# Cross-attention over heads on one Trainium2 core: rows ordered by token pairs, scores of 32x32 blocks, probabilities transposed by VectorE and placed on zeroed diagonals by ScalarE

## The chip, the cores and the metric

The kernel runs on one core of a Trainium2 chip. The metric is the device time of one execution in microseconds, the median of several runs. Of the core's engines the text speaks of TensorE (PE; its weight loads are PEld), VectorE (DVE), ScalarE (ACT), GpSimd (POOL) and SyncE (SP), which issues most DMAs.

## What is computed

4096 tokens of 512 numbers. For each token, attention runs over its own 16 heads: a 16x16 matrix of scores between the heads of the query and those of the key, a softmax over it, and a weighted sum of the value's heads. Tokens don't see each other. A layer of eight experts, two for each token, and a shared feed-forward part follow.

```python
Q = (q @ Wq.T + bq).reshape(bs, sl, H, HD)      # H, HD = 16, 32
K = (k @ Wk.T + bk).reshape(bs, sl, H, HD)
V = (v @ Wv.T + bv).reshape(bs, sl, H, HD)
score = jnp.einsum('bshd,bsgd->bshg', Q, K)
weight = jax.nn.softmax(score, axis=-1)
attn = jnp.einsum('bshg,bsgd->bshd', weight, V).reshape(bs, sl, nf)
return attn @ Wo.T + bo
...
x = x + xattn(layernorm(x), ctx, ctx, ...)
x = x + ffn(layernorm(x), ...)
```

## The kernel before

The code is written in blocks for each engine, with semaphores set by hand; each engine's order is the order of its code. The attention stage is a loop of 16 passes (NB) of 256 tokens (two halves s of 128). The passes are staggered: pass i projects keys, queries and values of block i + 1 (names K, Q, V, "ahead"), makes the attention of block i (S, T, P), and projects, adds and normalises what block i - 1 attended (O, Z, L, "behind"). PSUM banks are handed on through semaphores full and drained. Every matmul is recorded under the helper's line 728.

Scores. A query or key is split into three f16 parts of 32 rows, and rows 96 to 103 of q_st and k_st hold a mask, so that one matmul of 104 rows by 128 columns by 128 columns gives the scores of 8 tokens (GT) with all heads, and those between different tokens are pushed far down. 32 such matmuls make a pass, in 8 steps S00 to S13 of four. They stand between the pieces of the key and query projections (line 868 and on). VectorE takes the own token's score by a maximum over the 8 (line 1465), subtracts the row maximum; ScalarE takes the exponential; VectorE divides (line 1480, pr). GpSimd spreads pr to 128x128 with zeros outside the own token (line 1980, spread, 8 instructions a pass), TensorE transposes it (line 825, 32 a pass), ScalarE copies it to spread_t (line 1171, 8 a pass), and TensorE multiplies with v_p (attend, 32 matmuls on tiles of 32 columns, each recorded as two).

SyncE's queue in a pass (line 576): 16 loads of v_p from value_rows (line 518), which first wait until the store of value_rows has landed and P1 of the last pass is done; a piece of weights to be weighed; behind the wait for S13 (line 581) and k_low, 12 moves k_parts to k_st and, behind q_low, 12 moves q_parts to q_st (line 488); then x_sb, x_res, x_rows, z_rows, z_columns, the store of the next value_rows (line 505) and the load cx_in. All are issued in this order by one queue, and a wait holds up what stands behind it. Scores of pass i + 1 need k_st and q_st from pass i.

In the last pass SyncE issues, between the value store and the last v_p loads, the loads of the weights of the shared part (wsgu_in, wsdn_in) and of its first inputs. TensorE then begins the shared part, whose weights' low halves VectorE makes in the last pass (line 1509).

## Time and profile before

| | us |
|---|---|
| median of 3 runs (1491.32 to 1495.39) | 1491.42 |
| the profiled execution | 1494.03 |
| its span | 1492.3 |
| PE busy | 1404.3 (94%) |
| DVE busy | 911.3 (61%) |
| ACT busy | 647.1 (43%) |
| POOL busy | 503.7 (34%) |
| one pass of the attention loop, attend to attend | 36.33 |

The profile is one execution. Its timelines list instructions of one engine in order of time, with runs of the same instruction merged; a group's busy time is the union of its instructions. SyncE's rows (SPq) are the issues of DMAs, not their transfers. Attention lies between about 50 and 630 us, the shared part and the experts behind it.

### The profile page before, as it was taken

What the parts mean: (1) busy time and instruction counts of PE and PEld (TensorE: products, weight loads), DVE (VectorE), ACT (ScalarE), POOL (GpSimd) and SP (SyncE); (2) the same over time, 40 slices, a digit from 0 to 9 for tenths busy, and PEclk for the clock granted to TensorE, in tenths of its full rate; (3) what the DMA queues carried; (4) which work ended last, traced back from release to release, by engine and by line L of the source; (5) the groups of instructions that cost most, each with busy time, mean ns of one, the idle gap of its engine ahead of it and who ended that gap; (6) DMA issues with size and microseconds to landing.
All of it is one profiled execution on the core that took longest, in us unless ns stands there. A gap on an engine that the chain in (4) does not pass through costs nothing.

```text
span 1492.3 us, 33015 instructions
## 1 busy us (share of the span) xinstructions
PE 1404.3 (94%) x10387; PEld 1070.7 (72%) x10388; DVE 911.3 (61%) x1984; ACT 647.1 (43%) x1500; POOL 503.7 (34%) x607
## 2 busy tenths in 40 slices
PE   4899999999999999689899999999999999999997
PEld 4788888888888888557576756666666666666674
DVE  6888888888888887848765632222222222224666
ACT  6355555566665666532153523333333333332221
POOL 4444444444444442200567301111111111114554
PEclk9899999999999999789999999999999999999999
DMA  5556666666667886746855342222222222226996
GB/s 193 135 128 174 175 176 177 177 173 175 176 176 176 182 190 169 249 181 258 142 86 71 79 143 71 78 84 84 84 79 84 84 77 84 84 71 214 310 311 223
DMA packets 261893, 223.20 MB, mean 150 GB/s; under 512 B 182997, under 2 KB 191261, under 8 KB 261486
## 3 DMA queue, kind: packets, MB, share of 16 engines
q1 hardware_dynamic: 241224, 178.62, 42.9%
q0 software_dynamic: 12880, 35.47, 7.8%
q10 hardware_dynamic: 7734, 8.40, 1.9%
q8 instruction: 31, 0.51, 0.2%
q14 instruction: 24, 0.20, 0.1%
HBM read 129.30 MB, written 67.96 MB: 132 GB/s over the span
## 4 chain that ended last, share of the span: by engine, by line
PE 81%; DVE 8%; ACT 4%; issue 2%; DMA 2%; SPq 1%; POOL 1%; another core or an unknown queue 0%; DVEq 0%; POOLq 0%; ACTq 0%
PE psum_b L728 43%; PE psum_a L728 32%; PE psum_b L1044 2%; PE psum_a L825 2%; PE psum_b L1066 2%; ACT spread_t L1112 1%; DVE d_m L1728 1%; SPq L488 1%; PE psum_b L754 1%; DMA heads<-in_wk_t 1%; DVE wdn L1814 1%; DVE gate_act L1703 1%; ACT z_parts L1148 1%; DMA wgu_in<-base_rows 1%; PE psum_b L786 0%
## 5 line engine op out<-in xcount | busy, mean ns | idle before, releaser
L728 PE MATMUL psum_a<-wgu,zg_t 128*128 x1704 | 268.9, 315 | 1.9 <-DVE zg_t L1825 1.7
L1980 POOL TENSOR_TENSOR spread<-pr,own 128x512 f32<-128x512 f32 x128 | 136.7, 1099 | 302.9 <-DVE pr L1480 291.9
L728 PEld LDWEIGHTS psum_a<-wgu,zg_t 128*128 128x128 f16 x1704 | 167.3, 98 | 90.1 <-issue 10.1
L2054 POOL DMA_INDIRECT zg<-z_rows,gather_ix x71 | 67.2, 946 | 412.6 <-DVE gather_ix L1821 405.3
L728 PE MATMUL psum_a<-zt_in,wsgu 128*128 128x256 f16 x1536 | 170.6, 273 | 2.1 <-DVE wsgu L1509 1.3
L728 PEld LDWEIGHTS psum_a<-zt_in,wsgu 128*128 128x128 f16 x1536 | 148.9, 98 | 25.9 <-issue 7.6
L1830 DVE SCALAR_TENSOR_TENSOR silu<-psum_a,w_scale,silu 128x352 f32<-128x352 f32 x71 | 41.5, 584 | 194.9 <-ACT silu L1319 194.9
L728 PE MATMUL psum_b<-wsdn,sh_t 128*128 128x512 f16 (+1 forms) x576 | 135.6, 390 | 16.7 <-DVE sh_t L1709 16.2
L728 PE MATMUL psum_b<-wdn,act_t 128*128 (+1 forms) x639 | 149.6, 379 | 1.6 <-DVE act_t L1837 1.6
L1319 ACT ACTIVATE silu<-psum_a,w_scale 128x352 f32<-128x352 f32 x71 | 39.3, 553 | 203.7 <-PE psum_a L728 203.7
L728 PEld LDWEIGHTS psum_b<-wsdn,sh_t 128*128 128x128 f16 (+1 forms) x576 | 54.8, 99 | 91.8 <-issue 19.7
L728 PE MATMUL psum_b<-cx_t,wk 128*128 128x256 f32 x768 | 108.2, 297 | 6.4 <-DVE wk L385 6.2
L1112 ACT ACTIVATE at_raw<-psum_a 32x128 f32<-32x128 f32 x384 | 102.7, 267 | 22.8 <-PE psum_a L728 18.3
L1836 DVE TENSOR_TENSOR act_t<-psum_b,act_t 128x256 f16<-128x256 f32 x71 | 30.1, 425 | 129.5 <-ACT act_t L1112 129.5
L728 PEld LDWEIGHTS psum_b<-wdn,act_t 128*128 128x128 f16 (+1 forms) x639 | 62.5, 98 | 61.5 <-issue 1.9
L1262 ACT ACTIVATE gate_act<-psum_a,ws_scale 128x256 f32<-128x256 f32 x64 | 29.9, 469 | 176.7 <-PE psum_a L728 141.4
L728 PEld LDWEIGHTS psum_b<-cx_t,wk 128*128 128x128 f32 x768 | 100.7, 200 | 7.2 <-DVE wk L385 6.6
L728 PE MATMUL psum_b<-xn_t,wq 128*128 128x256 f32 x768 | 103.1, 287 | 0.0
L728 PE MATMUL psum_b<-wo,at_t 128*128 128x512 f32 x384 | 100.6, 416 | 0.0
L728 PE MATMUL psum_b<-wv,cx_t 128*128 128x512 f32 x384 | 94.2, 402 | 3.7 <-ACT q_parts L1120 3.7
L728 PEld LDWEIGHTS psum_b<-xn_t,wq 128*128 128x128 f32 x768 | 95.7, 192 | 0.1
L1112 ACT ACTIVATE spread_t<-psum_a 128x512 f32<-128x512 f32 x128 | 66.5, 620 | 63.4 <-PE psum_a L825 63.4
(247 smaller groups left out, 2516.5 us busy)
## 6 DMA issues: line engine op xcount, KB each, us to landing
expert_rows<-y_sb SPq DMA_DIRECT2D x71, 256.0 KB
k_st<-k_parts SPq DMA_DIRECT2D x192, 64.0 KB, 2.1
q_st<-q_parts SPq DMA_DIRECT2D x180, 64.0 KB, 2.1
...
```

The costliest lines, as they stand in the source:

```text
L488: sp.dma_start(dst[HD * n:HD * (n + 1), :, HD * l:HD * (l + 1), :].rearrange("p j m g -> p j (m g)"), parts[HD * l:HD * (l + 1), part].rea ...
L728: return nc.tensor.matmul(o, l, r, start=start, stop=stop)
L825: last = nc.tensor.transpose(bank_ap(step)[:, g * P:(g + 1) * P], spread[:, u * UG + g, :], ident[:, :])
L1044: last = nc.tensor.transpose(t_bank[:, kc * P:(kc + 1) * P], zg[:, b, kc * P:(kc + 1) * P], ident[:, :])
L1066: last = nc.tensor.transpose(a_bank[0:fn, f * P:(f + 1) * P], silu[:, b, f0:f0 + fn], ident[:, :])
L1112: return nc.scalar.activation(o, i_, ACT.Copy)
L1262: nc.scalar.activation(gate_act[at:at + fn, f % GB, :], sh_bank(f)[0:fn, 0:BT], ACT.Silu, scale=ws_scale[0:fn, 3:4]).then_inc(silu_ready, 1)
L1319: nc.scalar.activation(silu[:, b, :], psum_a[:, 2 * b * BANK:2 * b * BANK + F], ACT.Silu, scale=w_scale[:, 3:4]).then_inc(g_silu, 1)
L1830: V.scalar_tensor_tensor(out=silu[:, b, :], in0=psum_a[:, (2 * b + 1) * BANK:(2 * b + 1) * BANK + F], scalar=w_scale[:, 4:5], in1=silu[:, ...
L1836: V.tensor_tensor(act_t[:, b, LO, 0:2 * P], psum_b[1][:, 0:2 * P], act_t[:, b, HI, 0:2 * P], ALU.subtract)
L1980: G.tensor_tensor(spread[:, u * UG:(u + 1) * UG, :].rearrange("p r (g t) -> p r g t", t=GT), pr[:, s, u * UG:(u + 1) * UG, :].unsqueeze(3) ...
L2054: pool.indirect_dma_start(out=zg[:, b, :], out_offset=None, in_=z_d[:, :], in_offset=bass.IndirectOffsetOnAxis(ap=gather_ix[:, b:b + 1], a ...
```

## The change

Token t of 8, together with 16 groups g, now indexes the rows as (t, g), so that a 32x32 block of scores belongs to a pair of tokens (PAIR) with 16 heads each. Instead of one matmul for 8 tokens there are four of 32x32 on four column groups: 128 a pass in two steps, S0 and S1, of 64. The mask rows shrink from 8 to 2. The scores of a half fill one bank. VectorE takes a maximum over pairs (one instruction for a half), multiplies the exponentials by the inverse sums placed on the own token (own_inv, spread), and transposes within 32x32 blocks (turned). ScalarE copies the four strips of 32 partitions of turned to their places in spread_t (8 copies a pass), whose other elements GpSimd zeroes once, ahead of body 0. The transposes on TensorE and the spreading on GpSimd are gone. S0 stands behind the first half of the key projection, S1 behind the second, and normalise_out stands ahead of weigh_piece on VectorE. The loads of v_p keep their number (16) and bytes, but go to 16 partitions with a step of 2 rather than to 8 adjacent ones.

```diff
 MASK_Q, MASK_K = 2.0 ** 15, 65504.0
-ROWS = 3 * HD + GT
-GI = 4
-NJ = BT // (GT * GI)
+PAIR = 2
+NB32 = P // HD
+ROWS = 3 * HD + PAIR
+NJ = BT // (PAIR * NG)
...
-SCORES = [(f"S{s}{u}", f"A{u}") for s in range(SUB) for u in range(NU)]
-TURN_W = [[(f"T{s}{u}", f"A{u}") for u in range(NU)] for s in range(SUB)]
-FULL_PASS = (AHEAD + SCORES + AHEAD_KQ + OUT + TURN_W[0] + AHEAD_V + BEHIND + TURN_W[1] + ROUTE
+SCORES = [(f"S{s}", f"A{s}") for s in range(SUB)]
+FULL_PASS = (AHEAD + SCORES + AHEAD_KQ + OUT + AHEAD_V + BEHIND + ROUTE
...
-        q_st = sb("q_st", [ROWS, NJ, P, GI], F16, one)
-        k_st = sb("k_st", [ROWS, NJ, P, GI], F16, one)
+        q_st = sb("q_st", [ROWS, NJ, H, PAIR * NG], F16, one)
+        k_st = sb("k_st", [ROWS, NJ, H, PAIR * NG], F16, one)
...
-        spread = sb("spread", [P, NG, P], F32, one)
+        paired = sb("paired", [P, 2, SUB, NG * H * PAIR], F32, one)
+        spread, turned = paired[:, 0], paired[:, 1]
         spread_t = sb("spread_t", [P, SUB, NG * P], F32, one)
...
-                dst = at_raw[:, :, s * P:(s + 1) * P].rearrange("p c (j q t) -> p q c j t", q=GI, t=GT)[:, q]
+                dst = at_raw[:, :, s * P:(s + 1) * P].rearrange("p c (t j q) -> p q c j t", q=4, t=GT)[:, q]
...
-                src = v_d[bass.ds(i * BT, BT), :].rearrange("(n t) (c l d) -> l c t n d", t=GT, c=KC, l=4)
-                for l in range(4):
-                    for c in range(KC):
-                        at = (l * KC + c) * GT
-                        sp.dma_start(v_p[at:at + GT, :, :], src[l, c]).then_inc(v_moved, 16)
+                src = v_d[bass.ds(i * BT, BT), :].rearrange("(s t g) (h d) -> s t h g d", s=SUB, t=GT, h=H)
+                for s in range(SUB):
+                    for t in range(GT):
+                        at = t // PAIR * HD + t % PAIR
+                        sp.dma_start(v_p[at:at + HD - t % PAIR:PAIR, s * NG:(s + 1) * NG, :], src[s, t]).then_inc(v_moved, 16)
...
-                    wait_full(sp, "S13", i)
+                    wait_full(sp, "S1", i)
...
-            def scores(s, i, us):
-
-                for u in us:
-                    step = f"S{s}{u}"
-                    o = bank_ap(step)
-                    wait_free(pe, step, i)
-                    if s == 0 and u == 3 and not (isinstance(i, int) and i == 0):
-                        pe.wait_ge(half_out, i)
-                    if s == 0 and u == 0:
-                        pe.wait_ge(k_moved, (i + 1) * (3 * 4 * 16))
-                        pe.wait_ge(q_moved, (i + 1) * (3 * 4 * 16))
-                    for g in range(UG):
-                        n = s * NG + u * UG + g
-                        last = mm(o[:, g * P:(g + 1) * P], q_st[:, n // GI, :, n % GI], k_st[:, n // GI, :, n % GI], True, True)
-                    last.then_inc(full[BANK_OF[step]], 1)
-
-            def transpose_weights(s, i):
-                for u in range(NU):
-                    step = f"T{s}{u}"
-                    wait_free(pe, step, i)
-                    pe.wait_ge(spread_ready, i * (SUB * NU) + (s * NU + u + 1))
-                    for g in range(UG):
-                        last = nc.tensor.transpose(bank_ap(step)[:, g * P:(g + 1) * P], spread[:, u * UG + g, :], ident[:, :])
-                    last.then_inc(full[BANK_OF[step]], 1)
+            def scores(s, i):
+
+                step = f"S{s}"
+                wait_free(pe, step, i)
+                if s == 0:
+                    pe.wait_ge(k_moved, (i + 1) * (3 * 4 * 16))
+                    pe.wait_ge(q_moved, (i + 1) * (3 * 4 * 16))
+                for g in range(NG):
+                    for b in range(NB32):
+                        q_side, k_side = (st[:, s * NB32 + b].rearrange("p h (t g) -> p (h t) g", g=NG)[:, :, g] for st in (q_st, k_st))
+                        last = mm(bank_ap(step)[HD * b:HD * (b + 1), g * HD:(g + 1) * HD], q_side, k_side, True, True)
+                last.then_inc(full[BANK_OF[step]], 1)
 
             def attend(s, i):
 
                 step = f"P{s}"
                 wait_free(pe, step, i)
+                pe.wait_ge(spread_out, i * SUB + (s + 1))
                 if s == 0:
-                    for u in range(NU):
-                        wait_drained(pe, f"T1{u}", i)
-                    pe.wait_ge(v_moved, (i + 1) * (H * 16))
+                    pe.wait_ge(v_moved, (i + 1) * (SUB * GT * 16))
+                elif not (isinstance(i, int) and i == 0):
+                    pe.wait_ge(half_out, i)
...
-                scores(0, i, (1,))
                 if ahead:
                     project_k(i, (0, 1))
-                scores(0, i, (2,))
+                scores(0, i)
                 if ahead:
-                    project_k(i, (2,))
-                scores(0, i, (3,))
-                scores(1, i, (0,))
+                    project_k(i, (2, 3))
+                scores(1, i)
                 if ahead:
-                    project_k(i, (3,))
-                scores(1, i, (1,))
-                if ahead:
-                    project_q(i, (0,))
-                scores(1, i, (2,))
-                if ahead:
-                    project_q(i, (1,))
-                scores(1, i, (3,))
-                if ahead:
-                    project_q(i, (2, 3))
+                    project_q(i, range(KC))
                 if behind:
                     project_out(0, i)
                     project_out(1, i)
-                transpose_weights(0, i)
                 if ahead:
                     project_v(i)
                 if behind:
                     turn_z(i)
-                transpose_weights(1, i)
                 if behind:
                     route(i)
...
-                    scores(0, i + 1, (0,))
...
-                    src = bank_ap(step)[:, c * BT:(c + 1) * BT].rearrange("p (j q t) -> p j t q", j=NJ, q=GI)
-                    nc.scalar.activation(whole_[:, 2 * b + c, :].rearrange("p (j t q) -> p j t q", j=NJ, q=GI), src, ACT.Identity,
+                    src = bank_ap(step)[:, c * BT:(c + 1) * BT]
+                    nc.scalar.activation(whole_[:, 2 * b + c, :], src, ACT.Identity,
                                          bias=bias[:, 2 * b + c:2 * b + c + 1], scale=scale)
-                    last = nc.scalar.activation(parts[:, HI, :, 2 * b + c, :].rearrange("p j (t q) -> p j t q", q=GI), src, ACT.Identity,
+                    last = nc.scalar.activation(parts[:, HI, :, 2 * b + c, :], src.rearrange("p (j t) -> p j t", j=NJ), ACT.Identity,
...
-                for u in range(NU):
-                    step = f"T{s}{u}"
-                    wait_full(act, step, i)
-                    copy(spread_t[:, s, u * BANK:(u + 1) * BANK], bank_ap(step)).then_inc(drained[BANK_OF[step]], 1)
+
+                act.wait_ge(pair_turned, i * SUB + (s + 1))
+                placed = spread_t[:, s].rearrange("p (r b t) -> p b r t", b=NB32, t=PAIR)
+                for b in range(NB32):
+                    last = copy(placed[HD * b:HD * (b + 1), b], turned[HD * b:HD * (b + 1), s].rearrange("p (r t) -> p r t", t=PAIR))
+                last.then_inc(spread_out, 1)
...
+            act.wait_ge(spread_zeroed, 1)
...
-            def own_scores(i, s, us):
-
-                for u in us:
-                    step = f"S{s}{u}"
-                    wait_full(dve, step, i)
-                    ins = V.tensor_reduce(out=sc[:, s, u * UG:(u + 1) * UG, :],
-                                          in_=bank_ap(step).rearrange("p (r g t) -> p r g t", r=UG, t=GT), axis=X, op=ALU.max)
-                    ins.then_inc(drained[BANK_OF[step]], 1)
+            def own_scores(i, s):
+
+                step = f"S{s}"
+                wait_full(dve, step, i)
+                V.tensor_reduce(out=sc[:, s].rearrange("p g h -> p (g h)"), in_=bank_ap(step).rearrange("p (r t) -> p r t", t=PAIR),
+                                axis=X, op=ALU.max).then_inc(drained[BANK_OF[step]], 1)
...
-                V.tensor_tensor(pr[:, s], ex[:, s], row_inv[:, s, :].unsqueeze(2).broadcast_to([P, NG, H]), ALU.mult).then_inc(pr_ready, 1)
+                link(V.tensor_tensor(own_inv[:, s], row_inv[:, s, :].unsqueeze(2).broadcast_to([P, NG, PAIR]),
+                                     own[:, :].unsqueeze(1).broadcast_to([P, NG, PAIR]), ALU.mult))
+                link(V.tensor_tensor(spread[:, s].rearrange("p (g h t) -> p g h t", g=NG, t=PAIR), ex[:, s].unsqueeze(3).broadcast_to([P, NG, H, PAIR]),
+                                     own_inv[:, s].unsqueeze(2).broadcast_to([P, NG, H, PAIR]), ALU.mult))
+                if not (isinstance(i, int) and i == 0):
+                    dve.wait_ge(spread_out, (i - 1) * SUB + (s + 1))
+                V.transpose(turned[:, s], spread[:, s]).then_inc(pair_turned, 1)
...
-                own_scores(i, 0, range(2))
                 next_key_scale(i - 1)
                 if ahead:
                     x_low(i)
-                own_scores(i, 0, range(2, NU))
+                own_scores(i, 0)
...
-                own_scores(i, 1, range(2))
+                own_scores(i, 1)
+                shift(i, 1)
                 softmax(i, 0)
-                own_scores(i, 1, range(2, NU))
-                shift(i, 1)
...
-                for s in range(SUB):
-                    if s == 1 and ahead2:
-                        for half in range(SUB):
-                            inverse_std(half, stat_no(i + 2, 0, half))
-                    pool.wait_ge(pr_ready, i * SUB + (s + 1))
-                    for u in range(NU):
-                        if s == 1:
-                            wait_full(pool, f"T0{u}", i)
-                        elif not (isinstance(i, int) and i == 0):
-                            wait_full(pool, f"T1{u}", i - 1)
-                        G.tensor_tensor(spread[:, u * UG:(u + 1) * UG, :].rearrange("p r (g t) -> p r g t", t=GT),
-                                        pr[:, s, u * UG:(u + 1) * UG, :].unsqueeze(3).broadcast_to([P, UG, H, GT]),
-                                        own[:, :].unsqueeze(1).unsqueeze(1).broadcast_to([P, UG, H, GT]), ALU.mult).then_inc(spread_ready, 1)
+                if ahead2:
+                    for half in range(SUB):
+                        inverse_std(half, stat_no(i + 2, 0, half))
...
+            pool.wait_ge(wo_split, 1)
+            pool.wait_ge(limits_ready, 1)
+            settle(pool)
+            G.memset(spread_t[:, :, :], 0.0).then_inc(spread_zeroed, 1)
```

TensorE in a pass, from the key projection to the start of the query projection, before:

```order
L728 MATMUL psum_b<-cx_t,wk 128x256 x24
L371 REGISTER_ALU
L728 MATMUL psum_a<-k_st,q_st 128x128 x4
L728 MATMUL psum_b<-cx_t,wk 128x256 x12
L728 MATMUL psum_a<-k_st,q_st 128x128 x4
L371 REGISTER_ALU
L728 MATMUL psum_a<-k_st,q_st 128x128 x4
L728 MATMUL psum_b<-cx_t,wk 128x256 x12
L728 MATMUL psum_a<-k_st,q_st 128x128 x4
L375 REGISTER_ALU
L728 MATMUL psum_b<-xn_t,wq 128x256 x12
```

The same place in the change:

```order
L729 MATMUL psum_b<-cx_t,wk 128x256 x24
L809 REGISTER_ALU
L729 MATMUL psum_a<-k_st,q_st 32x32 x64
L372 ISA
L729 MATMUL psum_b<-cx_t,wk 128x256 x24
L729 MATMUL psum_a<-k_st,q_st 32x32 x64
L376 REGISTER_ALU
L729 MATMUL psum_b<-xn_t,wq 128x256 x48
```

The scores, which stood in eight groups up to the middle of the query projection and with their first group at the end of the pass before, are now in two groups that end ahead of it.

SyncE in a pass, from the last loads of v_p to the moves of keys and queries, before:

```order
L518 DMA v_p<-value_rows 8x32x32
L563 ISA
L563 DMA weigh_in<-in_wdn_t 128x2x512
L565 ISA
L565 DMA weigh_in<-in_wdn_t 96x512
L365 ISA
L492 ISA
L488 DMA k_st<-k_parts 32x8x128 x12
L488 DMA q_st<-q_parts 32x8x128 x12
```

The same place in the change:

```order
L519 DMA v_p<-value_rows 16x16x32
L564 ISA
L564 DMA weigh_in<-in_wdn_t 128x2x512
L566 ISA
L566 DMA weigh_in<-in_wdn_t 96x512
L493 ISA
L489 DMA k_st<-k_parts 32x8x128 x12
L489 DMA q_st<-q_parts 32x8x128 x12
```

The order of the queue is the same, the moves have the same shape, and the v_p loads have another.

VectorE from the second half's scores to the first half's probabilities, in the change:

```order
L1443 TENSOR_REDUCE sc<-psum_a 128x256
L1449 TENSOR_REDUCE row_max<-sc 128x16
L129 REGISTER_ALU
L1450 TENSOR_TENSOR sc<-sc,row_max 128x256
L1453 ISA
L1454 TENSOR_REDUCE row_sum<-sc 128x16
L129 REGISTER_ALU
L1455 RECIPROCAL row_inv<-row_sum 128x16
```

Before, two reductions of four stood on each side of the first half's softmax; now one stands ahead of it, and the shift of the second half with it. Behind the reciprocal come own_inv, the multiplication to 512 columns and the transpose.

## Rows read from the trace of the kernel before

**Rows 1.** The page: the span, and TensorE's busy time.

```profile
span 1492.3 us, 33015 instructions
...
PE 1404.3 (94%) x10387; PEld 1070.7 (72%) x10388; DVE 911.3 (61%) x1984; ACT 647.1 (43%) x1500; POOL 503.7 (34%) x607
```

**Rows 2.** Timeline of PE, one pass: start, length in us, engine, line, operation, count.

```profile
411.17 1.95 PE L728 MATMUL psum_a<-spread_t,v_p 128*32 128x128 f32 x64 [1.06 <-ACT spread_t L1112]
...
415.01 0.63 PE L728 MATMUL psum_a<-k_st,q_st 104*128 104x128 f16 x4
415.40 3.13 PE L728 MATMUL psum_b<-cx_t,wk 128*128 128x256 f32 x24
...
443.96 1.91 PE L825 MATMUL psum_a<-ident,spread 128*128 128x128 f32 x16
445.80 0.64 PE L728 MATMUL psum_b<-z_t,wgate 128*32 128x256 f32 x8
447.50 1.96 PE L728 MATMUL psum_a<-spread_t,v_p 128*32 128x128 f32 x64 [1.06 <-ACT spread_t L1112]
```

**Rows 3.** By stage: us, busy PE, PEld, DVE, ACT, POOL (instructions), clock, DMA share, GB/s.

```profile
411.17:447.50 36.33, 35.27 (x304) 31.77 (x304) 31.38 (x68) 22.00 (x57) 16.15 (x18) 1.00 0.65 178
...
415.40:423.00 7.60, 7.60 (x66) 7.45 (x64) 7.13 (x21) 6.50 (x20) 0.00 (x0) 1.00 1.00 378
```

**Rows 4.** Timeline of SyncE's queue in the loop.

```profile
154.47 0.39 SPq L479 DMA_DIRECT2D x_sb<-in_x  x1
...
415.42 1.08 SPq L505 DMA_DIRECT2D value_rows<-heads  x1
...
423.06 7.28 SPq L518 DMA_DIRECT2D v_p<-value_rows  x16
...
431.89 7.84 SPq L488 DMA_DIRECT2D k_st<-k_parts  x12
439.85 7.77 SPq L488 DMA_DIRECT2D q_st<-q_parts  x12
...
484.78 0.40 SPq L479 DMA_DIRECT2D x_sb<-in_x  x1
```

**Rows 5.** Waits of SyncE's queue, whole span: us in total, times, longest.

```profile
SPq L381 <- DMA value_rows<-heads: 64.5, 15, 5.5
...
SPq L381 <- PE psum_a L728: 10.9, 2, 8.7
```

**Rows 6.** Timeline of SyncE's queue in pass 0, which is outside the loop.

```profile
49.95 6.90 SPq L518 DMA_DIRECT2D v_p<-value_rows  x16
56.97 0.40 SPq L563 DMA_DIRECT2D weigh_in<-in_wdn_t  x1
57.41 0.46 SPq L565 DMA_DIRECT2D weigh_in<-in_wdn_t  x1
```

**Rows 7.** Groups by form: busy us, mean ns, idle before.

```profile
L1465 DVE TENSOR_REDUCE sc<-psum_a 128x64 f32<-128x512 f32 x128 | 82.3, 683 | 3.6 <-PE psum_a L728 3.0 <-DVE ws_scale L1490 0.2
...
L1112 ACT ACTIVATE spread_t<-psum_a 128x512 f32<-128x512 f32 x128 | 66.5, 620 | 63.4 <-PE psum_a L825 63.4
...
L728 PEld LDWEIGHTS psum_a<-k_st,q_st 104*128 104x128 f16 x512 | 50.3, 120 | 15.8 <-issue 10.0 <-ACT at_raw L1112 2.0
```

**Rows 8.** Line 518: durations of the issues, min/median/max ns.

```profile
L518 SPq DMA_DIRECT2D v_p<-value_rows x256: 277/278/6277, 50.0 to 621.2; - x128
```

**Rows 9.** Timelines of SyncE's queue and of PE at the loop's end.

```profile
589.59 0.39 SPq L596 DMA_DIRECT2D z_rows<-z  x1
...
594.43 0.37 SPq L505 DMA_DIRECT2D value_rows<-heads  x1
...
604.96 16.61 SPq L518 DMA_DIRECT2D v_p<-value_rows  x16
...
627.38 2.88 PE L728 MATMUL psum_a<-spread_t,v_p 128*32 128x128 f32 x64
...
632.13 5.40 PE L728 MATMUL psum_a<-zt_in,wsgu 128*128 128x256 f16 x48 [1.34 <-DVE wsgu L1509]
```

41 lines of the change are left out of this document (20 added, 21 removed).

## Prediction

> **What bounds the kernel now.** The page is read first: the span is 1492.3 us and TensorE is busy for 94% of it [rows 1]. The profiled execution took 1494.03 us, 1.7 us more than its span and 0.2% above the median of 1491.42 us; I make the sum as a difference inside the span and take it off the median. The change touches only the attention loop (16 passes, about 50 to 630 us) and its ends; the experts and the shared part behind it are the same code. The timeline of TensorE comes next: from one attend to the next it is 447.50 - 411.17 = 36.33 us [rows 2], and the table by stage gives for that pass PE 35.27, DVE 31.38, ACT 22.00 and POOL 16.15 us busy [rows 3]. So TensorE sets the pace, with one wait of 1.06 us for spread_t.
>
> The third view is the one that decides here: the timeline of SyncE's queue [rows 4]. One pass of it is a value store (415.42), a wait until it has landed, 16 loads of v_p (7.28 us), the piece of weights, 12 moves of k_st (7.84 us), 12 of q_st (7.77 us), and the loads and stores of x and z. Nothing in it stands still but for the landing of the value store: 64.5 us in 15 waits, 4.3 us each [rows 5]. That wait ends with the burst around it, in which the DMA engines are 1.00 busy at 378 GB/s [rows 3]. The load of x_sb, once a pass, starts at 154.47 and nine passes later at 484.78 [rows 4]: (484.78 - 154.47) / 9 = 36.70 us. The queue therefore goes at its own pace, and this is slower than TensorE's 36.33; TensorE could run ahead of it only because q_st had some microseconds in hand at the start. A TensorE that gets faster does not find its queries earlier.
>
> **TensorE's part.** Removed: 32 transposes of spread. 16 of them take 445.80 - 443.96 = 1.84 us, so 115 ns each, 3.68 us a pass [rows 2]. Removed: 32 score matmuls of 128 columns; four take 415.40 - 415.01 = 0.39 us [rows 2], 0.10 us each, 3.2 us a pass. Removed: the wait of 1.06 us. Added: 128 matmuls of 32x32. The nearest row is attend itself, whose tiles are also 32 columns wide: 64 instructions in 1.95 us less the tail of the last, 29 ns each [rows 2]. At that price they cost 3.8 us a pass. Bounds: 25 ns, below attend's, since each streams a quarter of its columns, to 98 ns, the price of the old score matmul. I take 29 ns because the tiling and the order over four column groups are the same. TensorE's work in a pass then falls to 36.33 - 3.68 - 3.2 - 1.06 + 3.8 = 32.2 us.
>
> The Trainium skill, SBUF — State Buffer, section "Door 1: The DMA port swizzle", says that a stride is free up to 8 elements of 16 bits, because SBUF is read in lines of 16 bytes. The new score operands step 16 elements, the old ones 4. By that rule the new matmuls would read each element from a line of its own, and by it alone the sum would sit nearer the upper bound than the lower.
>
> The row that bears on it: the old score operands, with step 4, already load in 120 ns [rows 7].
>
> **VectorE, ScalarE, GpSimd.** VectorE loses six of eight reductions of 128x512, 683 ns each [rows 7] and 0.64 us apart, 3.8 us, and the two multiplications to pr, 0.86 us. It gains two own_inv (0.2 us each, by its smallest operations), and two multiplications and two transposes of 512 columns; I price these four like the reduction of 512, 0.69 us (bounds 0.4 and 1.4, half and double speed). Its work falls from 31.4 to about 29.9 us; if its idle time of 36.33 - 31.38 = 4.95 us stays, the engines' own chain closes in 34.9 us a pass. ScalarE keeps eight copies of 512 columns; they took 620 ns from PSUM [rows 7] and are hidden, since ScalarE is busy for 22 of 36 us. Were they twice as long, two of them more would lie ahead of the second attend, 2 us, still below the queue's pace. GpSimd loses 8.5 us a pass that stood beside other work, and it gains one memset of 4096 columns ahead of body 0 (2 to 4 us), behind which ScalarE stands; that ends before the key scale that ScalarE waits for there anyway. Moving normalise_out ahead of weigh_piece lets z wait for GpSimd and gives z about 1 us earlier; both lie inside the 34.9.
>
> **SyncE's queue.** k_st and q_st go in the same 24 moves of the same shape. The 16 loads of v_p change from 8 partitions by 32 runs to 16 partitions by 16 runs, each run 128 bytes as before. A v_p load now takes 278 ns [rows 8], and without the loop's registers 16 take 6.90 us, 0.43 us apart; beside them a load to 128 partitions by 2 runs takes 0.40 us, and the next starts 0.44 us after it [rows 6]. I take that last distance: + 0.01 us a load, 0.16 us a pass, 2.4 us in 15 passes. Bounds: -0.05 us a load (it could become cheaper, fewer runs for each partition), + 0.11 us a load if the gap behind each load stays and only its 278 ns grow to the 395 of the other shape, and at the far end the 0.65 us of a k_st move [rows 4], + 0.2 us a load. This queue's pace is then 36.9 us a pass (bounds 35.9 and 40), above the 34.9 of the engines: **the 4 us that TensorE saves in each pass turn into a wait for q_st at scores(0)**, of about 3 us.
>
> **Where something is gained.** At the start SyncE waited twice for the last scores, 10.9 us in all [rows 5]. The new S1 comes earlier in the pass. The second wait (2.2 us) goes, of the first (8.7 us) I take 1.2 us, since k_low then comes last: 3.4 us. At the end of the loop the queue issued z_rows at 589.59 and reached its value store only at 594.43, because it stood behind z_parts [rows 9]. In the new loop z is ready long before the queue: z_rows at 589.59 - 3.4 + 2.4 = 588.6, the value store 1.5 us later at 590.1, 4.3 us earlier. Behind it come the weights of the shared part and then the 16 loads of v_p for the last pass, which fill 16.61 us because of those weights and end at 621.57 [rows 9]; now 617.3, landed some 3 us later (bounds 2 and 7) at 620.3. The last attend, at 627.38 before [rows 9], starts there: 7.1 us earlier. The other chain, through the two softmaxes, z and the low halves of wsgu (scores at 589.4 plus about 29 us, 618.5), is just hidden under it. Behind the attend comes the shared part (632.13), which is TensorE's own work and moves with it. The sum is -7.1 us: **1484 us**.
>
> **Rivals.** (A) **The v_p loads get dearer to issue**, on the same queue that sets the pace. For: each goes to twice as many partitions, and no row shows this shape. Against: the two distances of [rows 6] are equal. At +0.11 us a load it is 1.8 us a pass, 26 us in 15 passes in place of my 2.4: 1484 + 24 = 1508 us. The point from which it is slower than before is +0.04 us a load. The Trainium skill, DMA: Bandwidth & Descriptors, section "Why a DMA increments its semaphore by 16 and not by 1", has a load spread over as many DMA engines as divide its slowest sizes, which would be 8 before and 16 now; it gives no issue time for either.
>
> (B) **The 32x32 matmuls cost 60 ns and more** (the stride, or a refill between tiles). At 60 ns the scores take 7.7 us a pass. From the last query matmul through ScalarE, the low halves, the second softmax and z to attend, the pass then closes in about 39 us, 2 us above the queue: 1484 + 13 x 2 = 1510 us. It decides from about 45 ns on. Short waits of TensorE that lower its clock would push the same way.
>
> (C) **The queue is no limit**: the landing of the value store shortens, or the loads get cheaper, and the pass closes at the engines' 34.9 us. 14 passes x 1.4 us = 20 us and the tail: 1464 us. For: the wait of 4.3 us is a wait for bandwidth, not issue. Against: the burst around it carries the same bytes.
>
> (D) The change doesn't shorten TensorE's pass at all, since the tiles don't run side by side and a score matmul costs what it cost (98 ns, 12.5 us a pass): above 1540 us.
>
> **How the numbers follow.** The forecast case (queue's pace, v_p loads within 0.03 us of now) has 0.5, A 0.2, B 0.08, C 0.17, D 0.05. A measurement of this kernel can tell about 0.3% (4.5 us) from no change, so faster means below 1486.9. The forecast case lies at 1475 to 1493 by the bounds on the start, the landing and the loads; about three quarters of it is faster, hardly any slower. With C: faster 0.54, same 0.21, slower 0.25. The range takes in C and A: 1463 to 1510.
>
> **What would show it.** Right: in the loop the passes are 36.5 to 37.2 us apart; TensorE's busy time in a pass falls by 3 us and it waits 2 to 4 us for DMA q_st in each; SyncE waits only for value_rows; the v_p loads are 0.43 to 0.47 us apart; score matmuls 25 to 35 ns apart. Wrong: no wait for q_st and a pass below 36 us (C), v_p loads of 0.5 us and more (A), or score groups of 64 that take 3 us and more (B).

## The result: 1550 us, 58 us slower than before

The changed kernel takes 1550.1 us (median of 1546.2 to 1555.6), the kernel before 1491.6 us: 1.039 times as long, 95% interval 1.035 to 1.043. The prediction said 1484 us with a range of 1463 to 1510, and faster. It was wrong in sign and outside its range. The profiled execution took 1546.2 us, its span is 1544.5 us. Three of all executions of the kernels below fell into a slower state and are left out of the medians.

The page of the changed kernel: span, busy times, and the chain that ended last by engine and by line.

```profile
span 1544.5 us, 34518 instructions
...
PE 1362.4 (88%) x11395; PEld 1021.2 (66%) x11412; DVE 898.0 (58%) x1952; ACT 715.4 (46%) x1500; POOL 369.4 (24%) x480
...
PE 47%; SPq 29%; DMA 8%; DVE 7%; issue 6%; ACT 2%; POOL 1%; POOLq 0%; DVEq 0%; ACTq 0%
PE psum_a L729 25%; PE psum_b L729 18%; SPq L489 14%; SPq L519 10%; DMA value_rows<-heads 7%; PE psum_b L1019 2%; PE psum_b L1041 1%; DVE d_m L1708 1%; DVE wdn L1794 1%; DVE gate_act L1683 1%; DMA wgu_in<-expert_rows,pos_ix 1%; DMA heads<-in_wk_t 1%; DVE sh_t L1689 1%; SPq L480 1%; SPq L557 1%
```

TensorE has 42 us less work than before (1404.3 in [rows 1]), and the kernel is longer. 29% of the chain that ended last are issues of SyncE's queue: the moves of keys and queries (L489) and the v_p loads (L519). The same queue in the loop, one pass (to be laid beside [rows 4]):

```profile
409.75 0.39 SPq L480 DMA_DIRECT2D x_sb<-in_x  x1
...
413.66 1.49 SPq L506 DMA_DIRECT2D value_rows<-heads  x1
...
421.81 12.19 SPq L519 DMA_DIRECT2D v_p<-value_rows  x16
...
435.44 7.82 SPq L489 DMA_DIRECT2D k_st<-k_parts  x12
443.37 7.78 SPq L489 DMA_DIRECT2D q_st<-q_parts  x12
451.52 0.40 SPq L480 DMA_DIRECT2D x_sb<-in_x  x1
```

The moves of keys and queries take what they took. The 16 loads of v_p take 12.19 us; they took 7.28 us [rows 4]. That is 4.9 us a pass. Their duration, all 256 of them (shortest, median, longest in ns), where [rows 8] has 277/278/6277:

```profile
L519 SPq DMA_DIRECT2D v_p<-value_rows x256: 580/581/3588, 48.9 to 681.0; - x128
```

The load of x_sb starts at 120.35 and ten passes later at 533.92, so a pass takes 41.36 us; before it was 36.69. The two profiled executions are 52.2 us apart (1546.2 and 1494.0), and 10 x 4.67 = 47 us of them are made there. The next three sets of v_p loads take 10.4 us each for 7.0, 6.4 and 7.2 before, 10.6 us more in all, and some of that comes back: the last attend starts 55.9 us later than before (683.25 for 627.38), the end is 52.2 us later. TensorE in the same pass:

```profile
411.01 1.34 PE L729 MATMUL psum_a<-k_st,q_st 98*32 98x32 f16 x64 [2.01 <-DMA q_st<-q_parts]
...
442.30 1.08 PE L729 MATMUL psum_b<-z_t,wgate 128*32 128x256 f32 x8 [5.74 <-DVE z_parts L1476]
443.14 2.80 PE L729 MATMUL psum_a<-spread_t,v_p 128*32 128x128 f32 x64
...
452.75 1.35 PE L729 MATMUL psum_a<-k_st,q_st 98*32 98x32 f16 x64 [2.37 <-DMA q_st<-q_parts]
```

It waits 2.0 to 2.4 us for q_st at the first scores, at the low end of what the prediction said, and another 5.7 us for z_parts: VectorE stands at weigh_in there (3.0 us), whose load is behind the v_p loads in SyncE's queue. From 115 to 495 us the waits for z_parts are 51.0 us in 10, those for q_st 11.1 us in 8, so most of the wait is not where the prediction had it, though the same queue makes both. The scores are cheap, 64 of them in 1.34 us. SyncE itself waits for one thing only between 100 and 660 us:

```profile
SPq L382 <- DMA value_rows<-heads: 62.4, 13, 5.8
```

The change is slower by rival A (the v_p loads get dearer to issue), with a price outside the bounds that the prediction gave it.

### The profile page after: what moved, and what is told of

It reads as the page before. It is cut to its first block, busy times and chain, and to the rows that moved or that the text cites. A ratio compares the mean times of both kernels' runs of the same rounds, so it can differ in the third digit from the quotient of the medians.

```text
span 1544.5 us, 34518 instructions
## 1 busy us (share of the span) xinstructions
PE 1362.4 (88%) x11395; PEld 1021.2 (66%) x11412; DVE 898.0 (58%) x1952; ACT 715.4 (46%) x1500; POOL 369.4 (24%) x480
## 4 chain that ended last, share of the span: by engine, by line
PE 47%; SPq 29%; DMA 8%; DVE 7%; issue 6%; ACT 2%; POOL 1%; POOLq 0%; DVEq 0%; ACTq 0%
PE psum_a L729 25%; PE psum_b L729 18%; SPq L489 14%; SPq L519 10%; DMA value_rows<-heads 7%; PE psum_b L1019 2%; PE psum_b L1041 1%; DVE d_m L1708 1%; DVE wdn L1794 1%; DVE gate_act L1683 1%; DMA wgu_in<-expert_rows,pos_ix 1%; DMA heads<-in_wk_t 1%; DVE sh_t L1689 1%; SPq L480 1%; SPq L557 1%
## 5 line engine op out<-in xcount | busy, mean ns | idle before, releaser
L1087 ACT ACTIVATE at_raw<-psum_a 32x128 f32<-32x128 f32 x384 | 147.8, 385 | 54.5 <-PE psum_a L729 49.9
L1915 POOL TENSOR_SCALAR var_eps<-mv 128x1 f32<-128x1 f32 x64 | 22.8, 356 | 548.4 <-DVE mv L1375 390.3
L1240 ACT ACTIVATE gate_act<-psum_a,ws_scale 128x256 f32<-128x256 f32 x64 | 29.9, 469 | 177.8 <-PE psum_a L729 142.0
L729 PE MATMUL psum_b<-xn_t,wq 128*128 128x256 f32 x768 | 96.2, 285 | 0.0
L1310 ACT ACTIVATE y_sb<-psum_b,wd_scale 128x512 f32<-128x512 f32 x71 | 48.8, 687 | 102.3 <-PE psum_b L729 102.3
```

The costliest lines, as they stand in the source:

```text
L729: return nc.tensor.matmul(o, l, r, start=start, stop=stop)
L1087: return nc.scalar.activation(o, i_, ACT.Copy)
L1240: nc.scalar.activation(gate_act[at:at + fn, f % GB, :], sh_bank(f)[0:fn, 0:BT], ACT.Silu, scale=ws_scale[0:fn, 3:4]).then_inc(silu_ready, 1)
L1310: nc.scalar.activation(y_sb[:, b, :], d_bank[:, :], ACT.Copy, scale=wd_scale[:, 5:6]).then_inc(d_out, 1)
L1915: link(G.tensor_scalar_add(var_eps[:, col:col + 1], mv[:, col, 1:2], EPS))
```

## Experiments

"Theory Q" is that SyncE's queue sets the pace and the dearer v_p loads are the loss. "Theory R" and "D" came later, for what Q left over. "The ring" is the chain of engines that wait for each other in a pass, without SyncE's queue. A pass, below, is the mean distance of the loads of x_sb over ten passes of the loop, from the one profiled execution of each kernel. Some kernels do the same work with values or tokens in other places than the computation needs; their expectations say so. The kernel before, run beside them, took 1492.6 to 1496.3 us.

### One part undone, one part alone

The change with the v_p loads in their old form:

```diff
-                src = v_d[...].rearrange("(s t g) (h d) -> s t h g d", ...)
-                        sp.dma_start(v_p[at:at + HD - t % PAIR:PAIR, s * NG:(s + 1) * NG, :], src[s, t])
+                src = v_d[...].rearrange("(n t) (c l d) -> l c t n d", ...)
+                        sp.dma_start(v_p[at:at + GT, :, :], src[l, c])
```

> The changed kernel with the 16 v_p loads in the form of before (8 adjacent partitions by 32 runs of 128 bytes); everything else is the change's. It leaves out the right placing of the values, so what is attended is a mix of tokens, and nothing else. Theory Q (SyncE's queue sets the pace and the dearer v_p loads are the whole loss): v_p loads at 278 ns again, 0.44 to 0.46 us apart, a pass of 36.4 to 37.2 us, a wait for q_st at the first scores of 2 us or more, 1475 to 1492 us. Theory E (the other new costs, the at_raw copies of 385 ns and the spread copies of 688 ns, close the pass through TensorE and VectorE by themselves): v_p loads cheap, but passes of 38 us and more and above 1505 us. If the queue is no limit once the loads are cheap, passes of 34.9 us and 1464 us.

Measured: 1507.7 us, 1.008 times before (1.004 to 1.013). 42 of the 58 us are gone. But 1507.7 is above Q's range and a pass is 37.85 us. The passes are of two kinds. In some the queue goes through without a wait for the engines, 36.3 us; in others it waits for them:

```profile
303.41 0.40 SPq L480 DMA_DIRECT2D x_sb<-in_x  x1
...
314.86 7.29 SPq L519 DMA_DIRECT2D v_p<-value_rows  x16
322.40 0.40 SPq L564 DMA_DIRECT2D weigh_in<-in_wdn_t  x1
...
326.08 7.81 SPq L489 DMA_DIRECT2D k_st<-k_parts  x12
334.01 7.78 SPq L489 DMA_DIRECT2D q_st<-q_parts  x12
342.15 0.40 SPq L480 DMA_DIRECT2D x_sb<-in_x  x1
```

This pass takes 38.74 us, and before the moves of k_st the queue stands for 2.8 us (323.3 to 326.1), waiting for VectorE's k_parts. So the engines close later than the 34.9 us of the prediction, and there is a second cost. Theory E has a part in the result.

The other way round, the kernel before with the new loads alone:

> The kernel before with one part of the change alone: the 16 v_p loads go to 16 partitions with a step of 2, 16 runs of 128 bytes each. Its values stand in the places of the change, so what is attended is a mix of tokens. Theory Q: the loads take 580 ns and stand 0.76 us apart, SyncE's queue grows by 4.9 us a pass to 41.4 to 41.8 us, and the time by 14 or 15 times that less what TensorE's 36.3 us leave, 1555 to 1570 us: slower than the whole change. Theory E: the loads alone cost less than 2 us a pass, below 1520 us.

Measured: 1553.1 us, 1.038 (1.035 to 1.042), a pass of 41.63 us. Q holds: this one edit makes the kernel before as slow as the whole change. The 16 issues grew by 4.91 us (12.19 for 7.28) and the pass by 4.94 (41.63 for 36.69). A queue with slack would have hidden a part of it, so the queue of the kernel before had none. TensorE's own chain stood right beside it: in the loop of the kernel before TensorE never waited for q_st, only for spread_t (115 to 495 us: total us, times, longest):

```profile
PE psum_a L728 <- ACT spread_t L1112: 11.7, 11, 1.1
```

Its attends are 36.33 us apart there, and the queue, at 36.69, was using up a lead. In this run TensorE waits for q_st 27.5 us in 8 times in the same stretch. The whole change is 3 us faster than this one edit (1550.1 and 1553.1), which is within the spread of the runs.

### What makes the load dear

Three kernels with other shapes of load in the place of v_p's, four or five shapes each (32 KB a load unless said).

> The changed kernel with four shapes of v_p load, four loads each, all of 256 runs of 128 bytes: 8 adjacent partitions by 32 runs; 16 adjacent by 16; 16 with a step of 2 by 16; 8 with a step of 4 by 32. The values are misplaced. Theory N (the number of partitions, or of DMA engines that divide it, sets the issue): 278, 580, 580, 278 ns. Theory S (the step between partitions sets it): 278, 278, 580, 580 ns. A pass of about 39 us by N, since half of the loads are dear (36.7 + 8 x 0.3).

> The changed kernel with four other shapes of v_p load, 32 KB each: 16 adjacent partitions with 2 KB in one run each (2 loads); 8 adjacent by 32 runs of 128 bytes, the partitions 128 bytes apart in memory rather than 2 KB (2 loads); 32 partitions by 8 runs (4 loads); 64 partitions by 4 runs (8 loads). The values are misplaced. If the number of partitions sets the issue time: 580, 278, 580 or more, 580 or more ns (a load to 128 partitions takes 0.40 us in the kernel before, so it can't grow without end). If the number of runs counts too, the first is far below 580 ns. If the stride in memory counts, the second is 580 ns.

> The changed kernel with five other shapes of v_p load: 8 partitions with a step of 2 by 32 runs (4 loads); 16 adjacent partitions that begin at 40 and 56, which are no multiples of 16, by 16 runs (4); 32 adjacent partitions with 2 KB in one run each (2); 16 adjacent by 8 runs (4); 8 adjacent by 32 (2). The values are misplaced. If the step is what costs: over 500, 322, below 500, 250 to 322, 278 ns. If what costs is that a load reaches over more than 16 partitions: 278, 322, 560 to 610 whatever the runs, 322, 278 ns.

From the first, in order: 8 adjacent partitions by 32 runs, 16 adjacent by 16, 16 with a step of 2 by 16, 8 with a step of 4 by 32. The numbers are shortest, median and longest issue in ns.

```profile
L519 SPq DMA_DIRECT2D v_p<-value_rows x64: 277/297/6605, 48.7 to 644.1; - x64
...
L522 SPq DMA_DIRECT2D v_p<-value_rows x64: 316/322/2402, 50.3 to 648.8; - x64
...
L525 SPq DMA_DIRECT2D v_p<-value_rows x64: 580/604/1723, 52.1 to 651.2; - x64
...
L527 SPq DMA_DIRECT2D v_p<-value_rows x64: 677/697/745, 55.9 to 654.1; - x64
```

Theory S holds and N falls for these shapes: 16 partitions rather than 8 cost 40 ns, a step between them 260 to 420. From the third kernel, 8 partitions with a step of 2 by 32 runs, which reach over 15 partitions only:

```profile
L520 SPq DMA_DIRECT2D v_p<-value_rows x64: 665/703/4019, 48.8 to 640.6; - x64
```

So it is not the reach either. Nor is it the start partition: 16 adjacent ones from 40 or 56 on take 332 ns. The three kernels took 1521.9, 1521.5 and 1514.4 us, one run each. Adjacent partitions are not always cheap, though: in the second kernel 32 of them by 8 runs took 584 ns and 64 by 4 runs 564, while 16 and 32 with one run of 2 KB each took 370 and 395. In the third, 16 adjacent by 8 runs, half the bytes, took 374 ns, more than the 322 of 16 by 16; 250 to 322 was expected. The stride in memory does not matter (296 ns with 128 bytes between partitions). What the issuing hardware does with a step stays open; the price list is what the runs show. The Trainium skill, DMA: Bandwidth & Descriptors, section "Why a DMA increments its semaphore by 16 and not by 1", has the number of DMA engines follow from the slowest sizes. By it the loads of 8 partitions use 8 engines with or without a step. They took 278 and 703 ns here, so that number alone would not price the issue; how many engines a load used was not read from a trace.

### Cheap loads that are right

If the 32 rows of a pair's block of keys stand in the order (token, head) instead of (head, token), each load goes to 16 adjacent partitions. Only the order in which VectorE writes spread changes with it.

```diff
-                        sp.dma_start(v_p[at:at + HD - t % PAIR:PAIR, s * NG:(s + 1) * NG, :], src[s, t])
+                        sp.dma_start(v_p[t * H:(t + 1) * H, s * NG:(s + 1) * NG, :], src[s, t])
...
-   spread[:, s].rearrange("p (g h t) -> p g h t", ...), ex[:, s].unsqueeze(3)..., own_inv[:, s].unsqueeze(2)...
+   spread[:, s].rearrange("p (g t h) -> p g t h", ...), ex[:, s].unsqueeze(2)..., own_inv[:, s].unsqueeze(3)...
```

> The changed kernel, complete, with the rows of a pair's 32x32 block of keys ordered by token and then head, so that each v_p load goes to 16 adjacent partitions; only the order in which VectorE writes spread and the places of v_p change. Theory S (the step between partitions is the cost of the load): 322 ns a load, 8.0 us for 16, SyncE's queue at 37.0 us a pass, and the time that of the run with the loads of before or a little over it, 1508 to 1514 us. If the step did not matter in the whole kernel: 1550 us.

Measured: 1512.6 us, 1.010 (1.006 to 1.014), a pass of 37.90 us. As expected by S.

The same loads as they are, but issued by GpSimd (fetch_values moves from SyncE's body to the start of GpSimd's):

> The changed kernel, complete, with the 16 v_p loads as they are (step of 2) but issued by GpSimd's queue, which is idle for most of the loop. Theory Q: SyncE's queue falls to about 30 us a pass and is no limit; the ring of engines that the run with the loads of before showed, 37.8 us a pass, sets the pace: 1500 to 1512 us. If it was still the queue there in part, down to 1495 us. If GpSimd needs over 1.5 us for an issue, v_p comes last at attend: above 1530 us.

Measured: 1511.6 us, 1.010 (1.006 to 1.015), 38.04 us a pass. SyncE's queue has room now (it waits for TensorE and VectorE) and nothing more is gained, so what is left over is the engines' ring. GpSimd issues a load in 0.60 us (9.68 us for 16), with the step of 2.

### The second cost: the writes to at_raw

Behind attend, ScalarE copies the sums to at_raw in 24 pieces of 32x128, ahead of xn_t, on which VectorE's whole pass waits. Before the change 8 tokens stood side by side in at_raw; now each element stands 64 bytes from the last. The groups of both kernels, 115 to 495 us (busy time, mean ns of one | idle time before it):

```profile
L1112 ACT ACTIVATE at_raw<-psum_a 32x128 f32<-32x128 f32 x264 | 70.6, 267 | 12.9 <-PE psum_a L728 9.8
```

```profile
L1087 ACT ACTIVATE at_raw<-psum_a 32x128 f32<-32x128 f32 x235 | 90.6, 385 | 40.8 <-PE psum_a L729 38.1
```

24 x 118 ns = 2.8 us more between attend and xn_t in each pass. In the change alone this is hidden behind the queue. Theory R is that it holds the ring open once the queue is out of the way. The edit: at_raw keeps the old layout and VectorE reads it permuted when it makes at_t.

```diff
-                dst = at_raw[...].rearrange("p c (t j q) -> p q c j t", ...)[:, q]
+                dst = at_raw[...].rearrange("p c (j q t) -> p q c j t", ...)[:, q]
...
-                    raw = at_raw[:, :, s * P:(s + 1) * P]
+                    raw = at_raw[:, :, s * P:(s + 1) * P].rearrange("p c (g t) -> p c t g", t=GT)
```

> As the run with adjacent partitions, and at_raw keeps the layout of before (8 tokens adjacent), while VectorE reads it permuted when it makes at_t. Complete. Theory R (the 24 copies to at_raw, 9.4 us of ScalarE between attend and xn_t, hold the ring of engines open): copies at 267 ns again, 2.8 us a pass less on that ring, which then closes in about 35 us; SyncE's queue is last again with 37.0 us a pass, 1492 to 1500 us. Rival W (the clock, 0.91 in the loop, and the waits around z hold it, not the copies): within 5 us of the run with adjacent partitions. If VectorE pays for the permuted read what the copies paid for the write (four reads of 128x512 a pass), the gain is halved.

> As the run with GpSimd's queue, and at_raw in the layout of before with VectorE's permuted read. Complete. Theory R: with no queue at its limit the ring closes 2.8 us earlier, 34.9 to 35.5 us a pass, 1462 to 1475 us: faster than both kernels. Rival W: no more than 5 us below the run with GpSimd's queue.

Measured with adjacent loads on SyncE: 1497.8 us, 1.002 (0.998 to 1.006), 37.26 us a pass. With GpSimd's queue: 1494.2 us, 1.001 (0.997 to 1.005), 37.04 us a pass. The first is 15 us faster than without the edit, as R has it, with the queue as the floor at 37.0 us. The second gained 17 us where R had 36 to 50, since VectorE pays for the permuted read:

```profile
L386 DVE TENSOR_TENSOR at_t<-at_raw,at_t 128x512 fp32r<-128x512 f32 x20 | 23.2, 1159 | 0.7
...
L1491 DVE CAST at_t<-at_raw 128x512 fp32r<-128x512 f32 x20 | 13.5, 673 | 0.0
```

Before, these take 693 and 420 ns: 2 x (466 + 253) = 1.4 us a pass. That halves the gain, as the expectation for the first had it for this case.

The write alone, in the kernel before (only the first of the two edits, the other way round):

> The kernel before with one part of the change alone: at_raw is written in steps of 64 bytes. The tokens of what is attended are permuted, nothing is left out. Theory R: the 24 copies on ScalarE take 385 rather than 267 ns and the 8 on VectorE 379 rather than 291 ns, 2.8 us later to xn_t; TensorE and VectorE had under 1 us to spare there, so the pass grows by 1.5 to 2.5 us, 1510 to 1530 us. Rival W: ScalarE has room (busy for 22 of 36 us) and the time stays within 5 us.

Measured: 1530.5 us, 1.024 (1.021 to 1.027), 39.00 us a pass, 381 ns a copy. R holds; W falls, though ScalarE has room by its busy time. From attend to attend TensorE now takes 39.2 us (161.34 to 200.55) for 36.33: it loses all of the 2.8 us, so the kernel before had nothing to spare there either. The loads of x_sb show only 2.3 us more, because the queue's own 36.69 was the larger number before.

And neither cost: v_p loads on GpSimd's queue and at_raw written and read as before.

> The changed kernel with the v_p loads on GpSimd's queue and at_raw written as before (8 tokens adjacent) and read in a row, so that the change pays neither for its loads nor for its writes. The tokens of what is attended are permuted, nothing is left out. Its engines then close by their own chain, which the prediction put at 34.9 us a pass. From the run with the permuted read (37.4 us a pass): VectorE has 1.4 us less a pass, 36.0 us, 1470 to 1480 us. If the prediction's 34.9 us hold: 1455 to 1465 us. If TensorE's lower clock and its wait for z hold the pass at 37: above 1488 us.

Measured: 1458.3 us, 0.975 (0.971 to 0.980), 34.85 us a pass. One pass of it by the table of windows:

```profile
353.00:387.10 34.10, 31.06 (x368) 27.48 (x367) 29.47 (x66) 23.69 (x57) 16.91 (x27) 1.00 0.65 192
```

TensorE's busy time fell from 35.27 [rows 3] to 31.06 us and VectorE's from 31.38 to 29.47. The prediction had 32.2, 29.9 and a ring of 34.9 us. Against the run with the loads on GpSimd this is one edit, the places of at_raw, and it is worth 53 us and 3.2 us a pass: that is the second cost. I expected 36.0 us here, from the run with the permuted read less VectorE's 1.4; the prediction's own number was the better one. This pass is one of eight at a granted clock of 1.00; the two others, at 0.86, took 36.9 us (see The clock, below).

Is it the 64 bytes? The same copies, with the elements taken in another order, so that the writes step by 16 bytes:

```diff
-    dst = ....rearrange("p c (t j q) -> p q c j t", ...)   src = ....rearrange("p (j l c t) -> p l c j t", ...)
+    dst = ....rearrange("p c (t j q) -> p q c t j", ...)   src = ....rearrange("p (j l c t) -> p l c t j", ...)
```

> The changed kernel, complete, with the v_p loads on GpSimd's queue, and the same elements copied to at_raw in another order: the innermost index goes in steps of 16 bytes in the writes and 512 bytes in PSUM, where the change goes in steps of 64 bytes and 4 bytes. If the 385 ns are a price of the 64-byte step in the write: 267 to 300 ns a copy, the ring of the run that pays for neither (34.7 us a pass), 1458 to 1466 us. If any step but a run of adjacent elements costs it, or the 512-byte step in PSUM does: 385 ns or more, 1508 us and more.

Measured: 1513.5 us, 1.014 (1.012 to 1.016), 38.56 us a pass, 398 ns a copy. A step of 16 bytes is no better than one of 64. The Trainium skill, SBUF — State Buffer, section "Door 1: The DMA port swizzle", says that SBUF gives its full rate where consecutive accesses fall into the same line of 16 bytes. By it a step of 16 and one of 64 bytes cost the same for four-byte elements, and the trace agrees. PSUM was also read with a step of 512 bytes here, so the two are not told apart by this run alone.

### What is last then, and a version that is faster

In the run with GpSimd's queue and the permuted read, VectorE stands for 3.0 us a pass behind route and attend, for the turned logits, and TensorE for 2.7 us ahead of route. Theory D puts attend into that gap: ScalarE's second weights_out goes ahead of z_out, and attend ahead of turn_z.

```diff
+                attend(0, i)
+                attend(1, i)
                 if behind:
                     turn_z(i)
                 if behind:
                     route(i)
-                attend(0, i)
-                attend(1, i)
```

> As the run with GpSimd's queue and the permuted read, and both attends stand ahead of turn_z on TensorE, with ScalarE's second weights_out ahead of z_out. Complete. Theory D (the ring through VectorE is last: its 31.9 us of work a pass, 3.0 us in which it waits for the turned logits behind route and attend, and gaps between linked instructions): the wait of 3.0 us goes, a pass of 34 to 35 us in place of 37.4, TensorE's clock nearer to 1.00, 1445 to 1465 us. Rival: TensorE and ScalarE only wait in other places and the pass stays above 36.5 us, 1485 us and more.

> As the run before it, but at_raw as in the change (64-byte steps in the writes, reads in a row). Complete. The write costs ScalarE 2.8 us a pass more and VectorE 0.7 us more, the permuted read costs VectorE 1.4 us: if VectorE's work alone sets the pace, this is the faster of the two by 0.5 us a pass, 7 us; if ScalarE's at_raw copies are still on the ring, it is the slower by 15 to 25 us.

> The early attends and the permuted read, with the v_p loads on SyncE's queue again, to 16 adjacent partitions. Complete. Theory Q: the engines could close in 35 us, but SyncE's queue needs 37.0 us a pass, so nothing is gained over the run with adjacent partitions and permuted read, 1490 to 1500 us. If the queue was not the limit at 37: below 1475 us.

Measured, in this order: 1476.6 us (0.988, 0.985 to 0.991; 35.46 us a pass), 1479.8 us (0.991, 0.988 to 0.994; 35.88 us), 1503.1 us (1.007, 1.005 to 1.008; 37.10 us). Two versions beat the kernel before. D is right in sign: the pass is 1.6 us shorter, where I expected 2 to 3. Its mechanism is not shown alone, because the clock moved too: attend took 3.0 to 3.65 us in ten of eleven passes of the run with GpSimd's queue and the permuted read, and 1.95 us in every pass here. The second is slower than the first by 3 us only, between the two cases of its expectation: with attend early, ScalarE has time for most of the dear copies. The third shows the queue as the floor again, 37.1 us a pass, although the same engines close in 35.5; it is some us above its forecast and 5 us slower than the same kernel with the late attend. There the last attend waited 4.1 us for v_p; here it waits 18.4, and the shared part begins at 639.74 us rather than at 635.21:

```profile
PE psum_a L728 <- DMA v_p<-value_rows: 18.4, 1, 18.4
```

With attend early, TensorE is 80% of the chain that ended last, but VectorE is busy for 31 of the 35.5 us of a pass as well. Its 8 copies to at_raw go to ScalarE:

> As the fastest so far (early attends, GpSimd's queue, permuted read; 35.4 us a pass, of which VectorE is busy for 30.9 us and held by gaps between linked instructions for most of the rest), and the 8 copies to at_raw that VectorE makes (2.4 us a pass) go to ScalarE, which makes xn_t between the two halves. Complete. If VectorE is the limit: 33 to 34 us a pass, 1450 to 1462 us. If TensorE (33 us of work a pass) or ScalarE takes over: within 6 us of 1476 us.

Measured: 1480.2 us, 0.990 (0.985 to 0.995), 35.62 us a pass. Nothing gained: VectorE alone was not what was last. Whether it never was, or ScalarE lost with the copies what VectorE gained, this run does not tell apart.

TensorE's waits in the early version, by what they were for (us in all, times, longest):

```profile
PE psum_b L715 <- DVE z_parts L1462: 21.9, 15, 1.5
PE psum_b L715 <- DVE logits_t L1468: 18.0, 15, 1.3
```

The first goes if attend stands between turn_z and route:

> As the run before it, with both attends between turn_z and route on TensorE and ScalarE's second weights_out ahead of z_out. Complete. If the copies are cheap, TensorE's wait for z_parts ahead of route (2.7 us a pass) is filled by attend: 33 to 34 us a pass, 1445 to 1456 us. If TensorE is last already, as the early attends showed (32.5 us of work and 3 us of waits), no gain: 1466 to 1478 us.

Measured: 1466.1 us, 0.984 (0.981 to 0.987), 34.74 us a pass. It is the fastest complete version: the wait for z_parts falls to 6.5 us in all, and the dear copies are 5% of its chain or less. The pass is just above the first forecast and the time at the lower edge of the second. It is the change with v_p loads on GpSimd's queue, attend between turn_z and route, weights_out ahead of z_out, and the copies in the order of the run with steps of 16 bytes.

The last question was put to the kernel before, with its own v_p loads on GpSimd's queue:

> The kernel before, complete, with its v_p loads issued by GpSimd instead of SyncE. The premise of the prediction was that SyncE's queue sets the pace there, 36.7 us, just above TensorE's 36.33. If so, the pass falls to TensorE's 36.3 us and the time to 1480 to 1488 us, or less if TensorE could wait less too. Rival: GpSimd's 16 issues of 0.6 us stand ahead of its spread, which waits for nothing of theirs but order; if they come late, spread_t and with it attend wait, above 1495 us.

Measured: 1554.7 us, 1.041 (1.036 to 1.045), 39.99 us a pass. The rival came true, and this says nothing on the premise. GpSimd's timeline:

```profile
417.79 7.58 POOL L1966 DMA_DIRECT2D v_p<-value_rows  x11 [9.33 <-DMA value_rows<-heads]
428.10 3.30 POOL L1966 DMA_DIRECT2D v_p<-value_rows  x5 [2.74 <-issue]
431.42 4.16 POOL L1980 TENSOR_TENSOR spread<-pr,own 128x512 f32<-128x512 f32 x4
435.55 0.67 POOL L1921 TENSOR_SCALAR var_eps<-mv 128x1 f32<-128x1 f32 x1
```

The loads stand ahead of spread and of the rstd of the next x, and wait for value_rows. So where they stand here, GpSimd can take these loads only because the change took spread away from it; another place in its order was not tried. That is a gain of the change which the prediction had put at nothing ("loses 8.5 us a pass that stood beside other work").

## Why the prediction was wrong, point by point

**The bound.** Right in what matters here: SyncE's queue had no slack (the new loads alone: 4.91 us more in the queue, 4.94 in the pass). But it was one of two limits 0.4 us apart, and nothing else was free either: the dearer copies alone cost their whole 2.8 us. "Nothing in it stands still but for the landing of the value store" overlooks 3.3 us of waits for z_parts, in 6 times from 120 to 490 us.

**The v_p loads: the step that failed.** "I take that last distance: + 0.01 us a load". Measured + 0.31 us (12.19 - 7.28 = 4.91 us for 16). The bounds did not hold it either; the far end was + 0.2, from a k_st move. The two rows it was taken from ([rows 6]: 8 adjacent partitions by 32 runs, 128 adjacent by 2) bracket the number of partitions but have no step between them, and the step was the one new property of the shape. The prediction described the edit as "from 8 partitions by 32 runs to 16 partitions by 16 runs" and priced just that; this part alone costs 0.04 us (322 for 278 ns), within the bounds. The section on the change says "with a step of 2", and that did not reach the sum. The only row that was near, a k_st move, was used as the far end; its 611 ns are close to the 581 measured, by chance as far as is known, since no row of before shows a step. Rival A named the right term and a half-right reason (twice as many partitions). As the change turns slower from + 0.04 us a load on, a chance of 0.2 was too little for a shape without a row. The chances don't quite add up either: rival B's 1510 us is slower than before too, so slower should have had 0.33 and not 0.25.

**The writes to at_raw: a term that was missing.** The edit stands in the diff and in no sum. It costs ScalarE 2.8 us a pass (385 for 267 ns, 24 times) and VectorE 0.7 us (379 for 291 ns, 8 times). Behind the queue at 41.4 us it costs nothing that shows (the kernel before with the new loads and the cheap copies is no faster); without the dear loads a pass is 37.9 to 38.0 instead of 34.9 us. Had the loads cost what I said, the result would have been about 1508 us (the old loads in the change), not 1484, slower and not faster: the forecast would have missed its direction without rival A too. That 1508 is also rival A's number is chance.

**The engines' own chain.** Right in kind: 34.9 us forecast, 34.85 with neither cost, and 1458 us against the 1464 of rival C. TensorE's work was 31.06 for 32.2 us, VectorE's 29.47 for 29.9. That the ring agrees to 0.05 us is luck: the 34.85 are eight passes of 34.3 us and two of 36.9 at a lower clock, for which the sum had no term.

**The 32x32 matmuls.** Too dear in the forecast: 21 ns each (64 in 1.34 us) for 29, below the lower bound of 25. Rivals B and D are out. The prediction drew on the Trainium skill, SBUF — State Buffer, section "Door 1: The DMA port swizzle", which would have put them nearer the upper bound. Nothing of that size shows for these operands, whose elements are 32 bytes apart. One weight load takes 171 ns for the 120 of the old ones (115 to 495 us), though it is a quarter as wide; the loads overlap, and whether a part of the 21 ns is due to the step was not separated.

**ScalarE's copies to spread_t.** 687 ns for 620, four in 2.7 to 2.9 us for 2.06. Hidden, as said.

**The start and the end.** Of the 3.4 us at the start, the change with the old loads shows 1.5 (x_sb at 116.36 for 117.87). In the change SyncE still waits there for 4.1 us for the scores and 1.4 us for k_parts. At the end z_rows to value store fell from 4.84 us [rows 9] to 1.91 (650.02 to 651.93), 2.9 of the 3.3 us that I gave it. Both are small beside the loop.

**The clock.** The prediction named it as a push within rival B and gave it no number. In the change with the old loads, attend takes 2.8 to 3.65 us in eight of eleven passes and 1.94 in three, for 1.95 in every pass before:

```profile
460.39 3.65 PE L729 MATMUL psum_a<-spread_t,v_p 128*32 128x128 f32 x64
```

The granted clock is 0.50 there, the lower of its two levels (1.2 GHz), behind waits of 1.4, 1.4 and 2.7 us:

```profile
460.50:464.00 3.50, 3.50 (x69) 2.98 (x61) 1.19 (x4) 1.91 (x6) 0.00 (x0) 0.50 1.04 400
```

That is 1.7 us more for the same work. The waits just ahead do not decide it. In the run with neither cost the attends of two passes in a row stand behind the same wait of 2.68 us; in the first 64 matmuls take 1.94 us, in the second 32 do:

```profile
355.75 0.64 PE L715 MATMUL psum_b<-z_t,wgate 128*32 128x256 f32 x8 [2.68 <-DVE z_parts L1462]
356.20 1.94 PE L715 MATMUL psum_a<-spread_t,v_p 128*32 128x128 f32 x64
...
389.61 1.08 PE L715 MATMUL psum_b<-z_t,wgate 128*32 128x256 f32 x8 [2.68 <-DVE z_parts L1462]
390.46 1.94 PE L715 MATMUL psum_a<-spread_t,v_p 128*32 128x128 f32 x32
```

What the clock costs can be read by sorting the ten passes of a run by their mean granted clock. Both runs have the loads on GpSimd's queue (mean us of a pass):

| | at 1.00 | at 0.84 to 0.91 |
|---|---|---|
| copies as in the change | 36.8 (3 passes) | 38.7 (6 passes) |
| copies as before | 34.3 (8 passes) | 36.9 (2 passes) |

One more pass of the first, at 0.95, took 37.4 us. The means come from one execution of each kernel. A lower clock goes with 1.9 to 2.6 us more a pass, and at equal clock the copies cost 1.8 to 2.5 us. So of the 3.2 us between the two means (38.04 and 34.85) I estimate 2.0 to 2.4 for the copies by themselves and 0.8 to 1.2 for the clock, which is low in more of the passes. Why it is low more often there stays open. In the kernel before TensorE waited 1.06 us a pass and its clock stayed at 1.00; with waits of 2.7 us and more, as in the changed kernels, it was 0.50 in some stretches. So a change that takes work from TensorE and leaves waits between its parts can give some of the gain back by the clock.
